# Two double banks for the turning of the first stage, one for its mixing, and a chunk's statistics taken by ScalarE

## The reference, cut to what matters

```python
def _gn(v, G=32, eps=1e-05):
    g = v.reshape(B_, H_, W_, G, C_ // G)
    m = jnp.mean(g, axis=(1, 2, 4), keepdims=True)
    s = jnp.var(g, axis=(1, 2, 4), keepdims=True)
    return ((g - m) / jnp.sqrt(s + eps)).reshape(v.shape)

def _L0_conv_ref(x, centers, spreads, bias):   # mixes the 128 positions, a softmax map for each of 4 heads
    posmap = jax.nn.softmax(pos_score, axis=1)
    out = jnp.einsum('mns,bwnvs->bwmvs', posmap, x.reshape(b, w, n, v, s))
    return (out + bias[None, :, :, :, None]).reshape(b, w, n, c)

def _L1_conv_ref(x, W):                        # a scan over the 64 rows
    def step(carry, row):
        new = row + jax.nn.relu(conv1d_same(carry, W))   # 9 taps, 64 channels to 64
        return (new, new)
    ...

x = x + _L0_conv_ref(_gn(x), ...)              # x1, the first result
x = x + _L1_conv_ref(_gn(x), W)
```

## Time and profile before

| | |
|---|---|
| median of three runs | 761.73 us (758.88 to 762.5) |
| the profiled execution's own time | 760.53 us |
| its span in the trace | 758.7 us |
| first stage, to the scan's first carry | 0 to 184 us |
| share of the span busy: TensorE, VectorE, ScalarE, GpSimd | 89%, 79%, 65%, 58% |

### The profile page before, as it was taken

The page is one execution under the profiler, slowest core; times in us unless marked ns, Lnnn a source line. Parts: engine busy times, 40 slices in busy tenths (PEclk is TensorE's granted clock), DMA queues, the critical chain, the costliest instruction groups (busy, mean ns, idle before and its releaser), DMA issues.

```text
span 758.7 us, 18279 instructions
## 1 busy us (share of the span) xinstructions
PE 672.7 (89%) x5044; PEld 639.8 (84%) x5044; DVE 597.2 (79%) x1426; ACT 491.5 (65%) x854; POOL 438.6 (58%) x480
## 2 busy tenths in 40 slices
PE   1577777765999999999899999996999999999995
PEld 1466665655999999999799999996999999999995
DVE  7579999983898878896979888785676777777774
ACT  1156777676676867767586777775666666666661
POOL 1555556651666756765576767843655555555554
PEclk9889999995999999999999999997999999999998
DMA  9955656231455555554555643322444444444444
GB/s 183 165 111 112 137 114 135 60 76 37 74 108 106 106 90 104 108 102 78 106 109 103 110 83 52 55 46 48 72 74 77 72 69 69 75 74 72 69 74 79
DMA packets 412050, 68.18 MB, mean 90 GB/s; under 512 B 411988, under 2 KB 411988, under 8 KB 411988
## 3 DMA queue, kind: packets, MB, share of 16 engines
q1 hardware_dynamic: 359764, 61.17, 44.2%
q10 hardware_dynamic: 52224, 6.30, 5.4%
HBM read 33.85 MB, written 33.55 MB: 89 GB/s over the span
## 4 chain that ended last, share of the span: by engine, by line
PE 52%; DVE 18%; SPq 12%; issue 9%; ACT 4%; DMA 2%; POOL 1%; ACTq 1%; DVEq 0%; POOLq 0%
PE ps_conv L1080 27%; PE ps_conv L1084 13%; SPq L311 11%; PE ps_mix L973 6%; DVE st L632 5%; PE ps_in L986 4%; DVE x_sb L726 3%; DVE st L733 2%; ACT x_paired L490 2%; DVE carry L846 1%; PE ps_small L963 1%; DVE staged L833 1%; DMA x_sb<-in_x_dram 1%; DVE carry_l L856 1%; DVE rows L726 1%
## 5 line engine op out<-in xcount | busy, mean ns | idle before, releaser
L409 POOL TENSOR_TENSOR total<-x_paired,carry 128x256 f32<-128x256 f32 (+1 forms) x256 | 238.4, 931 | 221.4 <-DVE staged L833 213.7
L544 ACT ACTIVATE carry_h<-carry 128x256 fp32r<-128x256 f32 x252 | 105.3, 418 | 172.5 <-DVE carry L846 124.7
L1080 PE MATMUL ps_conv<-carry_h,wh 128*128 128x256 f32 x1260 | 202.3, 291 | 5.9 <-ACT carry_h L544 5.7
L518 ACT ACTIVATE rows<-x_paired,shift,rstd 128x256 f32 (+1 forms) x240 | 200.9, 844 | 0.3 <-issue 0.2
L1084 PE MATMUL ps_conv<-carry_l,wh 128*128 128x256 f32 x1260 | 191.0, 282 | 1.1 <-DVE carry_l L856 1.1
L1080 PE MATMUL ps_conv<-carry_h,wl 128*128 128x256 f32 x1260 | 191.1, 282 | 0.0
L856 DVE TENSOR_TENSOR carry_l<-carry,carry_h 128x256 fp32r<-128x256 f32 x252 | 141.1, 560 | 56.8 <-ACT carry_h L544 41.7
L490 ACT ACTIVATE x_paired<-ps_in,shift 64x512 f32<-64x512 f32 (+1 forms) x240 | 164.1, 684 | 23.7 <-PE ps_in L986 19.9
L1080 PEld LDWEIGHTS ps_conv<-carry_h,wh 128*128 128x128 f32 x1260 | 168.6, 190 | 11.1 <-ACT carry_h L544 8.9
L1084 PEld LDWEIGHTS ps_conv<-carry_l,wh 128*128 128x128 f32 x1260 | 167.9, 189 | 1.5 <-DVE carry_l L856 1.3
L1080 PEld LDWEIGHTS ps_conv<-carry_h,wl 128*128 128x128 f32 x1260 | 168.7, 190 | 0.0
(11 more groups left out here) (95 smaller groups left out, 346.7 us busy)
## 6 DMA issues: line engine op xcount, KB each, us to landing
x_sb<-in_x_dram SPq DMA_DIRECT2D x52, 512.0 KB, 4.1
out_dram<-staged SPq DMA_DIRECT2D x832, 32.0 KB, 1.6
rows<-in_x_dram SPq DMA_DIRECT2D x12, 512.0 KB, 4.0
out_dram<-staged ACTq DMA_DIRECT2D x192, 32.0 KB, 1.8
x_paired<-in_L_conv_W_dram SPq DMA_DIRECT2D x2, 80.0 KB, 2.8
x_paired<-in_L_conv_W_dram SPq DMA_DIRECT2D x2, 64.0 KB, 2.6
x_paired<-v_attention_centers_dram SPq DMA_DIRECT2D x1, 0.0 KB
x_paired<-v_attention_spreads_dram SPq DMA_DIRECT2D x1, 0.0 KB
```

What stands on the lines that cost most here:

```text
L409: ins = nc.gpsimd.tensor_tensor(summed[:, w0:w0 + n, :], x1_rows(wave, it, i, 1, s * WS + w0, n)[:, 0, :, :], carried[:, w0:w0 + n, :], AL ...
L518: nc.scalar.activation(rows[:, g % 2, :, w // WS, :, w % WS], x1_rows(wave, it, g * RG, RG, w, 1)[:, :, 0, :], ACT.Identity, scale=rstd2[: ...
L1080: nc.tensor.matmul(ps_conv[:, s * BANK:s * BANK + SW], w[:, d, :], carry_h[s][:, d:d + J, :].rearrange("p j w -> p (j w)"), start=(w is wh ...
```

## The change

The first stage's mixing has `ps_mix` alone, so that a chunk's mixing waits for the eviction of the chunk right before it. The turning has two double banks instead: even chunks go to `ps_conv`, odd ones to `ps_in` (`turned_in`), and the turning of chunk n waits until chunk n - 2 has been kept. Before the scan uses `ps_conv`, TensorE waits until all but the last chunk have been kept.

For batches 0 to 6 ScalarE takes x1's statistics of chunk 2. The four keeping instructions of that chunk also give a sum along their elements (`accum_out`), into `sums2`. After it has kept chunk 3, ScalarE runs `squares2`: it makes two means out of the sums, in one small instruction, and then two instructions take the sums of squared deviations from these means, over 512 elements of 128 partitions each; what they write elementwise goes to `staged`, which nothing uses yet. All of it is laid down in `st2` as the statistics instruction would have left it, the counts by one `memset` at the start. The two `stats2` of chunk 2 that VectorE did around the next batch's chunk 0 fall away, `moments2` waits for `squares2`, and batches use `st2`'s slots 0 to 6 and 1 to 7 in turn. Batch 7 keeps its statistics on VectorE, and the scan is as it was.

```diff
+        def turned_in(n):
+
+            return ps_conv if isinstance(n, int) and n < W * CH and n % 2 == 0 else ps_in
...
-            def keep_in(b, k, wave, bw, c, first, count, free):
+            def keep_in(b, k, wave, bw, c, first, count, free, sums=None):
...
                 for r, q in ((0, 0), (0, 1), (1, 0), (1, 1))[first:first + count]:
-                    src = ps_in[r * C:(r + 1) * C, :].rearrange("p (k j q) -> p q k j", k=HR, q=2)
+                    src = turned_in(b * CH + c)[r * C:(r + 1) * C, :].rearrange("p (k j q) -> p q k j", k=HR, q=2)
                     ins = nc.scalar.activation(dst[q * C:(q + 1) * C, r:CR:2, :], src[:, q, :, :],
-                                               ACT.Identity, bias=shift1[r * C:(r + 1) * C, k:k + 1])
+                                               ACT.Identity, bias=shift1[r * C:(r + 1) * C, k:k + 1],
+                                               accum_out=None if sums is None else sums[q * C:(q + 1) * C, r:r + 1])
...
+            def squares2(b):
+
+                slot = (TU - 1) * (b % 2)
+                act.wait_ge(in_kept, b * CH + CH - 1)
+                if b > 1:
+                    act.wait_ge(mv_ready, b - 1)
+                nc.scalar.activation(st2[:, slot, 1:6:3], sums2[:, :], ACT.Copy,
+                                     scale=1.0 / (HR * J)).then_inc(mean_c_ready, 1)
+                act.wait_ge(mean_c_ready, b + 1)
+                for r in range(2):
+                    nc.scalar.activation(staged[:, r, :], x1_chunk(0, b, CH - 2)[:, r:CR:2, :],
+                                         ACT.Square, scale=-1.0, bias=st2[:, slot, 1 + 3 * r:2 + 3 * r],
+                                         accum_out=st2[:, slot, 2 + 3 * r:3 + 3 * r]).then_inc(squares2_done, 1)
...
             for b in range(W):
                 if b > 0:
                     keep_in(b - 1, (b - 1) % 2, 0, b - 1, CH - 1, 0, 4, None)
+                    squares2(b - 1)
                 dev2_of(b + 1)
...
-                keep_in(b, b % 2, 0, b, 2, 0, 4, None)
+                if b > 0:
+                    act.wait_ge(squares2_done, 2 * b)
+                keep_in(b, b % 2, 0, b, 2, 0, 4, None, sums2 if b < W - 1 else None)
...
+            nc.vector.memset(st2[:, 0:TU:TU - 1, 0:6:3], HR * J)
...
+                slot = 2 * c + u
+                if shares(b):
+                    slot = 2 * min(c, CH - 2) + u + 1
+                nc.vector.bn_stats(st2[:, slot, :], x1_unit(wave, bw, c, u)).then_inc(stats2_done, 1)
 
             def moments2(b):
...
+                if shares(b):
+                    dve.wait_ge(squares2_done, 2 * (b + 1))
                 dve.wait_ge(stats2_done, seen)
-                nc.vector.bn_aggr(mv[:, :], st2[:, :, :].rearrange("p n k -> p (n k)")).then_inc(mv_ready, 1)
+                nc.vector.bn_aggr(mv[:, :], st2[:, first:last, :].rearrange("p n k -> p (n k)")).then_inc(mv_ready, 1)
...
                 e = buf_of(b)
-                mix_to_x1(b, e, c, (ps_mix, ps_conv)[c % 2])
+                mix_to_x1(b, e, c, ps_mix)
...
                     stats1(nb, ne, 9, 4)
-                    if b > 0:
-                        stats2(b - 1, 0, b - 1, 2, 0)
-                        stats2(b - 1, 0, b - 1, 2, 1)
                     stats1(nb, ne, 13, 3)
...
                 pe.wait_ge(x1_done, n + 1)
-                if not is_zero(n):
-                    pe.wait_ge(in_kept, n)
+                two = isinstance(n, int) and n < W * CH
+                if not (two and n < 2):
+                    pe.wait_ge(in_kept, n - 1 if two else n)
...
                     turn_in(b, e, CH - 1)
+                    pe.wait_ge(in_kept, W * CH - 1)
...
                 for m in range(2):
-                    mix_half(b, c, m, (ps_mix, ps_conv)[c % 2], n - 1 if n >= 2 else None)
+                    mix_half(b, c, m, ps_mix, n if n >= 1 else None)
```

More of the change, by code:

```diff
@@ L95, in mix_and_scan_kernel @@
         st2 = sb("st2", [P, 2 * CH, 6])
+        sums2 = sb("sums2", [P, 2])
         mv = sb("mv", [P, 2])
@@ L186, in mix_and_scan_kernel @@
         stats2_done = sem("stats2_done")
+        mean_c_ready = sem("mean_c_ready")
+        squares2_done = sem("squares2_done")
         mv_ready = sem("mv_ready")
@@ L727, in mix_to_x1, with shares @@
                                                bias_col[:, 0:1], v, ALU.add, ALU.add).then_inc(x1_done, 1)
+            def shares(b):
+                return isinstance(b, int) and b < W - 1
             def stats2(b, wave, bw, c, u):
@@ L732, in stats2 @@
                 dve.wait_ge(in_kept, b * CH + c + 1)
-                nc.vector.bn_stats(st2[:, 2 * c + u, :], x1_unit(wave, bw, c, u)).then_inc(stats2_done, 1)
+                slot = 2 * c + u
+                if shares(b):
+                    slot = 2 * min(c, CH - 2) + u + 1
+                nc.vector.bn_stats(st2[:, slot, :], x1_unit(wave, bw, c, u)).then_inc(stats2_done, 1)
             def moments2(b):
-                seen = held(dve, TU * b + TU)
+                first, last = 0, TU
+                seen = held(dve, TU * b + TU - 2 * (W - 1))
+                if shares(b):
+                    seen = (TU - 2) * (b + 1)
+                    first, last = b % 2, TU - 1 + b % 2
                 alone(dve, consts)
+                if shares(b):
+                    dve.wait_ge(squares2_done, 2 * (b + 1))
                 dve.wait_ge(stats2_done, seen)
-                nc.vector.bn_aggr(mv[:, :], st2[:, :, :].rearrange("p n k -> p (n k)")).then_inc(mv_ready, 1)
+                nc.vector.bn_aggr(mv[:, :], st2[:, first:last, :].rearrange("p n k -> p (n k)")).then_inc(mv_ready, 1)
             def deviations2(b, wave):
@@ L981, in turn_in @@
                 pe.wait_ge(x1_done, n + 1)
-                if not is_zero(n):
-                    pe.wait_ge(in_kept, n)
+                two = isinstance(n, int) and n < W * CH
+                if not (two and n < 2):
+                    pe.wait_ge(in_kept, n - 1 if two else n)
                 for k in range(HR):
                     at = c * CC + 2 * k * C
-                    ins = nc.tensor.transpose(ps_in[:, k * P:(k + 1) * P], x_bufs[e][:, at:at + P], ident[:, :])
+                    ins = nc.tensor.transpose(turned_in(n)[:, k * P:(k + 1) * P], x_bufs[e][:, at:at + P], ident[:, :])
                 ins.then_inc(in_turned, 1)
```

## The result

The changed kernel took 751.75 us (median of four runs, 750.26 to 754.82) against 762.12 us for the kernel before (median of four, one run more than ahead of the prediction), a ratio of 0.9862 with a 95% interval of 0.9834 to 0.9891. In two later comparisons with the kernel before, on chips 11 and 12, the same kernel gave 0.9896 (0.9867 to 0.9925) and 0.9879 (0.9843 to 0.9914). The profiled execution took 750.49 us, 10.0 less than the one of before.

The account below looks back on a forecast made before the run. VectorE was taken to bound the first stage. Six batches (7.4 us), start (1.0) and end (1.1) gave 9.5 off the profiled 760.5, so 751.0; with runs' median 1.2 higher, 751.5 was forecast, range 747.0 to 757.0.

Parts of the forecast that it names:

- two loops that tie: First stage, per batch: VectorE's 15.58 us and ScalarE's 15.96 at most nearly tie, 15.8 taken.
- squares of about 0.7 us: ScalarE's two new squares behind chunk 3: 0.69 us each plus 0.10 for a reading, 1.58 for both.
- no wait at `dev_c`: VectorE, second normalisation's small step: the 0.32 us wait goes, thanks to the turning's second bank.
- chunk 2 kept right behind the small square: ScalarE: keeping chunk 2 starts at 7.1 us after keeping chunk 0 began, not 8.2.
- VectorE's loop: VectorE's batch in the first stage: 17.03 - 1.18 - 0.32 + 0.05 = 15.58 us.
- ScalarE's loop: ScalarE's batch in the first stage, counted from keeping chunk 0: 15.96 us, or a little less.
- A batch: Batches 1 to 6 of the first stage: 15.8 us instead of 17.03, 1.23 less each, 7.4 in six.
- the third rival: Single mixing bank turns against it: at the lower clock a mixing takes 3.59, a batch 20.2, total about 778; chance 0.06.
- two of the signs that I named: TensorE's clock at 1.00; VectorE waits a few tenths for ScalarE at chunk 0's statistics if ScalarE's loop is longer.
- The start: Between batches 0 and 1, earlier turning and mixing, less VectorE work: gain 1.0 us, bounds 0.5 and 2.6.
- The end: Behind the last batch, keeping (7, 2) no longer waits for its turning: gain 1.1 us, bounds 0.9 and 1.3.
- The rivals of a ScalarE at 16.7 or 17.3: Dearer squares lengthen ScalarE's batch: 16.7 us, total about 757, chance 0.21; or 17.3, 760.9, no change, chance 0.13.

Follow-up runs that it names:

- e3: Mixing cut to one double bank, turning and statistics as before, against the kernel before: 763.11 us, ratio 0.9965.
- e4: Four more unused squares of 256 elements on ScalarE behind each batch's chunk 3, against the changed kernel: 763.66 us, ratio 1.0019.
- e2: Changed kernel with one bank for the turning and two for the mixing, so only the statistics move: 769.08 us, ratio 1.0059 (1.0032 to 1.0085).
- e10: Changed kernel with eight unused transposes of the identity behind the turning of chunk 3: 752.86 us, ratio 0.9863.
- e1: Only the banks change (two for the turning, one for the mixing), statistics stay on VectorE, against the kernel before: 758.81 us, ratio 0.9881.

## Why the prediction was right

The time (751.5 forecast, 751.75) and the mechanism of the batch were right: two loops that tie, squares of about 0.7 us, no wait at `dev_c`, and chunk 2 kept right behind the small square. That the number came so near is luck in part, since terms were off in both directions and cancelled.

- **VectorE's loop** was 15.47 us where 15.58 was forecast. The removed pair is worth its 1.18. The wait at `dev_c` was worth its 0.32 or more: from the reciprocal ahead of it to the step behind it was 0.72 us before and is 0.26 to 0.40 now. The mixing cost 0.14, not 0.05 (e3): it started 0.06 later and took 1.97 us, where I had left it at 1.89. The lines of before and of batch 3 after:

```profile
112.38 0.34 DVE L697 RECIPROCAL guess<-std 128x32 f32<-128x32 f32 x1
...
113.10 0.15 DVE L746 TENSOR_SCALAR minus_mean<-ps_out 128x1 f32<-128x1 f32 x1
```

```profile
88.90 0.34 DVE L723 RECIPROCAL guess<-std 128x32 f32<-128x32 f32 x1
89.15 0.10 DVE L784 TENSOR_TENSOR dev_c<-mv,ps_out 128x1 f32<-128x1 f32 x1
89.17 0.15 DVE L785 TENSOR_SCALAR minus_mean<-ps_out 128x1 f32<-128x1 f32 x1
```

- **ScalarE's loop** was forecast at 15.96 at most, and is about VectorE's 15.47. The squares with their readings took 0.72, not 0.79; the readings in the keeping held the next instruction back by 0.1 to 0.2 us each, a little over my bound of 0.19, and were hidden in the wait ahead of chunk 3, as forecast; 0.3 to 0.7 us of that wait is left. That ScalarE's loop has no room is shown (e4); that VectorE's has none is read from its timeline, where 0.38 us is the one wait. That ScalarE's time could be used only with the second bank is shown by e2.
- **A batch** on the mean was (150.27 - 54.42) / 6 = 15.98 between the keepings of chunk 0, near the 15.8 taken, but for another reason: four batches at 15.5 and two lengthened by the clock. Six batches gave 6.4 us where 7.4 was forecast. That lower clock is the third rival's mechanism, mis-placed: I argued that earlier turnings only shorten gaps, and gave it all batches or none. It came in part, at about 2.7 us, by the 120.0 us here and the 117.3 in e10, where the clock held. At the upper clock a batch gains 1.56, where I had 1.23, and the fall hid that. So two of the signs that I named failed: the clock was not 1.00 throughout, and VectorE waited for ScalarE at chunk 0's statistics only behind a fall of the clock. The wait for the mixing stayed at 0.38 us or less in these batches. What keeps the clock at 1.00 stays open: it held in batches 1 to 6 of the kernel before with gaps of 1.7 us, with more work in the gaps, and with the turning first and no work added.
- **The start** is the term that was mis-sized most: 3.4 us (57.80 to 54.42) against 1.0 with bounds of 0.5 and 2.6. Of it 1.2 is the removed pair, and `squares2`, counted at 0.5, cost nothing there. The mixing of (1, 0) ran at the upper level, so that the eviction's wait of 1.49 us went: 1.6, which my bound of 2.6 allowed for. The last 0.6 is an earlier eviction of (0, 2), behind a mixing that still takes 3.05 us. e3 has the faster mixing of (1, 0) with the single mixing bank alone, e2 with the statistics alone, so it needs neither the second turning bank nor the single mixing bank. Only one execution of the kernel before has a trace, and in the changed kernel the start differs by 1.5 us from one execution to the next, so how much of these 2.2 us the change brings is not shown. The line of the changed kernel:

```profile
46.76 1.97 PE L1009 MATMUL ps_mix<-xs,mix 128*128 128x256 f32 x8
```

- **The end** gave 1.2 (24.19 to 22.97 from keeping (7, 0) to the first carry's copy), 1.1 forecast. The stage's sum was 9.5 forecast and 11.0 measured, and the scan's 1.0, which I had counted as nothing and which lies within its scatter, brought the total back.
- The rivals of a ScalarE at 16.7 or 17.3 fell with the squares at 0.72. The `memset`, bounded at 0.3, takes 0.06 us.

## What to carry to other kernels

Idle time of an engine is not yet time to give work to: look at what ends each of its waits, and free that first. Here the statistics alone made the kernel slower and with a second bank for the turning they made it faster by more than the sum of the parts. One bank is enough for a product whose consumer has other work between two evictions that is longer than release and product together (about 2.15 us here; where it is shorter, the rest is a wait, 0.38 us at one place of four); the bank that this frees belongs where two engines hand one buffer to and fro. Before dealing out one engine's work anew, follow every in-order queue on the way: a small product that waited for ScalarE undid two such versions here.

## What was not expected of the hardware

TensorE's granted clock fell in the same batch in three executions out of three, with 12.9 us of TensorE work in a 15.5 us batch, while the kernel before held 1.00 in batches 1 to 6 with 12.65 us in 17.03. The amount of work doesn't tell the two apart: e2 fell in batch 5 with 12.7 us in the 17.6 of each batch before it, and e1 held with 12.9 in 16.65. Nor does the length of a gap alone: e4 fell in batch 1 behind one of 2.60 us and held in later batches with 2.56 to 2.82. With eight transposes more in a batch, in either gap, it held at 1.00, in one profiled execution each. A stall of VectorE of 0.32 us by the profile was worth up to 0.46 us when it went (0.72 to 0.26 us from the reciprocal to the step behind `dev_c`, in the batch at 57.97 us): without the wait, `dev_c` starts at 89.15 in the lines above, before the reciprocal has ended at 89.24.
